# Attention outputs turned before they are normalised, border sums in four portions, and a re-ordered last head

## What is computed

```python
x = x + attention(group_norm(x, 32 groups))
x = x + conv_block(group_norm(x, 32 groups))
# attention: q, k, v = W x + b, block-diagonal over 8 heads of 16 channels;
#   softmax(q^T k / 4) over 1024 x 1024 positions in each head; times v; projection Wp, bias bp
# conv_block: depthwise 7 x 7 convolution, padding 3, bias; LayerNorm over the 128 channels
#   (gain, shift); dense 128 -> 512, exact GELU, dense 512 -> 128
```

## Time and profile before

| | |
|---|---|
| median of three runs | 354.29 us |
| profiled execution, and its span | 350.4 us, 348.6 us |
| TensorE busy | 312.3 us (90%) |
| VectorE busy | 262.3 us (75%), of it 150.6 in the maxima, 24.5 in reciprocals from SBUF |
| ScalarE busy | 174.3 us (50%) |
| GpSimd busy | 89.8 us (26%) |
| mean granted TensorE clock | 0.926 |
| chain of waits | TensorE 54%, VectorE 32%, GpSimd 6% |

### The profile page before, as it was taken

How to read it: one execution, slowest core, us unless ns; L and a number is a source line. 1 busy time by engine, 2 the same in 40 slices (tenths; PEclk the granted TensorE clock), 3 DMA queues, 4 the chain that set the end, 5 groups by cost and what they waited for, 6 DMA issues and landing times.

```text
span 348.6 us, 5518 instructions
## 1 busy us (share of the span) xinstructions
PE 312.3 (90%) x2095; PEld 139.4 (40%) x2095; DVE 262.3 (75%) x273; ACT 174.3 (50%) x347; POOL 89.8 (26%) x96
## 2 busy tenths in 40 slices
PE   7999999938999999997699799799997899997896
PEld 3453644413454454452244344344333343422232
DVE  2758759845989989987498778998997239997621
ACT  1315548724877777765367447677325262201132
POOL 6102262991000000000005175978401010100110
PEclk9999859985999999999889659999999599999999
DMA  6273011211221232123011223770000002641001
GB/s 197 48 120 84 1 24 25 37 19 19 37 53 23 37 53 39 24 50 53 0 26 31 47 87 56 176 148 8 5 8 0 0 8 57 147 113 69 0 5 56
DMA packets 10538, 17.34 MB, mean 50 GB/s; under 512 B 3588, under 2 KB 5764, under 8 KB 10512
## 3 DMA queue, kind: packets, MB, share of 16 engines
q1 hardware_dynamic: 10320, 16.60, 22.0%
q10 hardware_dynamic: 192, 0.39, 0.7%
HBM read 5.00 MB, written 1.73 MB: 19 GB/s over the span
## 4 chain that ended last, share of the span: by engine, by line
PE 54%; DVE 32%; POOL 6%; issue 3%; DMA 2%; ACT 2%; SPq 1%; DVEq 0%; POOLq 0%
PE ps L1022 13%; PE ps L1033 13%; DVE mx L738 13%; PE ps L978 7%; DVE hl L782 6%; DVE rden L748 5%; PE ps L1121 4%; POOL inside L531 4%; DVE on L750 3%; PE ps L928 2%; PE ps L954 2%; PE ps L1186 2%; PE ps L1200 2%; PE ps L1145 2%; ACT pr L654 1%
## 5 line engine op out<-in xcount | busy, mean ns | idle before, releaser
L738 DVE TENSOR_REDUCE mx<-ps 128x1 f32<-128x1024 f32 x128 | 150.6, 1218 | 36.5 <-PE ps L978 36.2
L654 ACT ACTIVATE pr<-ps 128x512 f32<-128x512 f32 x256 | 134.8, 600 | 77.2 <-PE ps L1022 76.8
L1022 PE MATMUL ps<-qs,ks 50*128 50x512 f32 x256 | 104.5, 473 | 9.8 <-DVE xs L764 4.0
L978 PE MATMUL ps<-ks,qs 48*128 48x512 f32 x256 | 102.9, 471 | 5.6 <-DVE mx L738 5.6
L1033 PE MATMUL ps<-pr,va 128*32 128x256 f32 x1024 | 77.1, 424 | 0.0
L1022 PEld LDWEIGHTS ps<-qs,ks 50*128 50x128 f32 x256 | 46.8, 201 | 64.7 <-ACT pr L654 34.3
L978 PEld LDWEIGHTS ps<-ks,qs 48*128 48x128 f32 x256 | 45.4, 199 | 21.8 <-DVE mx L738 15.4
L1033 PEld LDWEIGHTS ps<-pr,va 128*32 128x32 f32 x1024 | 28.4, 117 | 36.2 <-ACT pr L654 15.4
L500 POOL CAST mparts<-mx 128x8 fp32r<-128x8 f32 x16 | 3.1, 191 | 152.3 <-DVE mx L738 152.3
L782 DVE SCALAR_TENSOR_TENSOR hl<-xpad,w,hl 128x512 f32<-128x512 f32 (+1 forms) x43 | 40.1, 934 | 1.2
L1121 PE MATMUL ps<-xr,wt 128*32 128x512 f32 x256 | 29.5, 595 | 1.6 <-DMA xr<-xpad 1.6
(11 more groups left out here) (97 smaller groups left out, 213.2 us busy)
## 6 DMA issues: line engine op xcount, KB each, us to landing
qs<-hl SPq DMA_DIRECT2D x48, 64.0 KB, 2.4
ks<-hl SPq DMA_DIRECT2D x42, 64.0 KB, 2.4
xr<-xpad SPq DMA_DIRECT2D x16, 95.0 KB, 2.1
xr<-pad_dram SPq DMA_DIRECT2D x4, 361.0 KB, 5.8
xr<-pad_dram SPq DMA_DIRECT2D x4, 304.0 KB, 5.2
xr<-xpad SPq DMA_DIRECT2D x16, 76.0 KB, 2.1
oc<-on SPq DMA_DIRECT2D x60, 16.0 KB, 1.8
xs<-x SPq DMA_DIRECT2D x2, 256.0 KB, 3.1
```

The source lines that it names most:

```text
L654: nc.scalar.activation(pr[:, n % PR, c * HALF:(c + 1) * HALF], bank("half", n, c), ACT.Exp, scale=SCALE).then_inc(exp_done, 1)
L738: nc.vector.tensor_reduce(mx[:, s % 2, i:i + 1], sm[(NT * s + i) % 2], AX.X, ALU.max).then_inc(max_done, 1)
L978: last = nc.tensor.matmul(sm[k % 2][:, c * HALF:(c + 1) * HALF], qs[rows, cell_of(s) + i * P:cell_of(s) + (i + 1) * P], ks[rows, cell_of(s ...
L1022: nc.tensor.matmul(bank("half", n, c), ks[rows, cell_of(t) + j * P:cell_of(t) + (j + 1) * P], qs[rows, cell_of(t) + c * HALF:cell_of(t) + ...
```

## The change

- **Normalising.** `denominators` becomes `turn_u`: two transposes of 128 x 128 put positions on the partitions, so that `rden` has 8 numbers a partition and the product is 128 x 128 elements, written in `ot` (positions x channels). `spread`, `wlast`, `on`, `collect` and their transfers go.
- **Image 0's projection.** Two more uses of banks, ("oc", 0) at (8, 6) and ("oc", 1) at (9, 0): four transposes each of `ot`, copied by ScalarE into `oc`. The projections stand at (9, 2) and (9, 6); ScalarE empties them with the bias. GpSimd adds x in `pad_image` and copies the sum to `x1`.
- **Border sums.** The 14 additions come in four portions, after `split_max` of 2, 3, 4 and 5.
- **Taps of image 0.** TensorE does 8 runs instead of 7 (16 pieces in head 14 instead of 14), VectorE 9 taps instead of 12.
- **Head 15.** `centre_out` at j = 1 (was 3), `ln_var` at 3 (was 6), `ln_turn` at 5 (was 7), `ln_scale` at 7 (was after the head). VectorE applies the scale before it normalises head 15. Three of the eight half blocks of the first dense layer stand between the last head and the projection of image 1, which is now eight transposes, two copies and two matmuls.
- **Three more `keep_busy` matmuls** after each of the first two blocks of head 0.
- **Image 1.** Eight of the 32 `fill_directly` transfers go to ScalarE's queue; VectorE's taps around `conv_sum(1)`, `ln_diag(1)` and `ln_apply(1)` are cut in other portions.

```diff
-PE_RUNS = (7, 9)
-DVE_TAPS = (12, 17)
+PE_RUNS = (8, 9)
+DVE_TAPS = (9, 17)
-FINISH = {(HEADS + 1, 0): ("proj", 0), (HEADS + 1, 2): ("proj", 1), (T - 2, 5): ("mean",), (T - 1, 0): ("var",)}
+FINISH = {(HEADS, 6): ("oc", 0), (HEADS + 1, 0): ("oc", 1), (HEADS + 1, 2): ("proj", 0), (HEADS + 1, 6): ("proj", 1),
+          (T - 2, 5): ("mean",), (T - 1, 0): ("var",)}
...
             def pad_image():
...
-                nc.gpsimd.tensor_copy(inner, image(x1[:, 0, :])).then_inc(S("xpad", 0), 2)
+                nc.gpsimd.tensor_tensor(inner, image(xs[:, 0, :]), image(oc[:, 0, :]), ALU.add).then_inc(S("xpad", 0), 2)
+                g.wait_ge(S("xpad", 0), 2)
+                nc.gpsimd.tensor_copy(image(x1[:, 0, :]), inner).then_inc(S("x1", 0), 1)
...
             split_max(2)
-            taps_inside()
-            for s in range(3, HEADS + 4):
+            taps_of_rows()
+            split_max(3)
+            taps_inside(0, 3)
+            split_max(4)
+            taps_inside(3, 6)
+            split_max(5)
+            taps_inside(6, KS)
+            for s in range(6, HEADS + 4):
                 split_max(s)
...
+            def copy_oc(c):
+                a.wait_ge(S("ot_T", 0), c + 1)
+                nc.scalar.activation(oc[:, 0, c * HALF:(c + 1) * HALF], bank("oc", c), ACT.Copy).then_inc(S("oc", 0), 1)
+
+            def copy_proj(c):
+                a.wait_ge(S("bout"), 1)
+                a.wait_ge(S("projp", 0), c + 1)
+                nc.scalar.activation(oc[:, 0, c * HALF:(c + 1) * HALF], bank("proj", c), ACT.Identity, bias=bout[:, 0:1])\
+                    .then_inc(S("projected"), 1)
...
-            also = {T - 1: {4: lambda: ln_square(0), 5: lambda: ln_centred(0)}}
+            also = {HEADS: {6: lambda: copy_oc(0)}, HEADS + 1: {0: lambda: copy_oc(1), 2: lambda: copy_proj(0), 6: lambda: copy_proj(1)},
+                    T - 1: {2: lambda: ln_square(0), 3: lambda: ln_centred(0)}}
...
             copy_u(T - 1)
-            gelus(0)
+            gelus(0, 0, 1)
+            a.wait_ge(S("ot_T", 1), 1)
+            nc.scalar.activation(oc[:, 1, 0:HALF], lower[:, 0:HALF], ACT.Copy).then_inc(S("oc", 1), 1)
+            gelus(0, 1)
+            fill_directly(nc.scalar, 1, range(SHIFTS // 2, SHIFTS))
...
-                nc.vector.reciprocal(rden[:, r, :], den_of(t)).then_inc(rd_ready, 1)
+                nc.vector.reciprocal(rden[:, r, :, :], otp_of(t)[:, :, :, D]).then_inc(rd_ready, 1)
                 v.wait_ge(rd_ready, t + 1)
-                nc.vector.tensor_tensor(on[:, r, :], u[:, r, :], rden[:, r, :], ALU.mult).then_inc(ot_done, 1)
+                nc.vector.tensor_tensor(
+                    ot[:, :, t * D:(t + 1) * D].rearrange("p (q k) d -> p q k d", k=2),
+                    otp_of(t)[:, :, :, 0:D],
+                    rden[:, r, :, :].rearrange("p q (k a) -> p q k a", a=1).broadcast_to([P, 4, 2, D]), ALU.mult).then_inc(ot_done, 1)
...
-            def denominators(t):
+            def turn_u(t):
                 t_.wait_ge(u_ready, t + 1)
-                t_.wait_ge(S("spread"), 1)
-                nc.tensor.matmul(ut_of(t), spread[:, :], u[:, t % 2, :], start=True, stop=True).then_inc(ot_ready, 1)
+                for i in range(2):
+                    last = nc.tensor.transpose(ut_of(t)[:, i * P:(i + 1) * P], u[:, t % 2, i * P:(i + 1) * P], ident)
+                last.then_inc(ot_ready, 1)
...
+                    if n < 2:
+                        keep_busy(3)
...
-                if kind == "proj":
-                    for r in range(2):
-                        t_.wait_ge(S("collected", r), 64 * HEADS // 2)
+                if kind == "oc":
+                    t_.wait_ge(ot_done, HEADS)
+                    for i in range(NT // 2):
+                        last = nc.tensor.transpose(bank("oc", *of)[:, i * P:(i + 1) * P], ot[:, of[0] * NT // 2 + i, 0:P], ident)
+                    last.then_inc(S("ot_T", 0), 1)
+                elif kind == "proj":
+                    t_.wait_ge(S("oc", 0), of[0] + 1)
...
-            head(T - 2, [(5, first_bias)] + [(3 + n // 3, *quads[n]) for n in range(2 * units)])
-            head(T - 1, [(3, centre_out, 0), (6, ln_var, 0), (7, ln_turn, 0)])
+            head(T - 2, [(5, first_bias)] + [(3 + n * 5 // (2 * units), *quads[n]) for n in range(2 * units)])
+            head(T - 1, [(1, centre_out, 0), (3, ln_var, 0), (5, ln_turn, 0), (7, ln_scale, 0)])
             times_v(NT * T - 2)
             times_v(NT * T - 1)
...
+            mlp(0, 0, 0)
+            turn_u(T - 1)
+            mlp(0, 0, 1)
             t_.wait_ge(ot_done, T)
...
+            for i in range(NT):
+                last = nc.tensor.transpose(lower[:, i * P:(i + 1) * P], ot[:, i, P:2 * P], ident)
+                if i % (NT // 2) == NT // 2 - 1:
+                    last.then_inc(S("ot_T", 1), 1)
+            mlp(0, 1, 0)
+            for c, done in enumerate((S("oc", 1), S("oc_low"))):
+                t_.wait_ge(done, 1)
+                nc.tensor.matmul(lower[:, c * HALF:(c + 1) * HALF], vec(C_WP, P), oc[:, 1, c * HALF:(c + 1) * HALF],
+                                 start=True, stop=True).then_inc(S("projp", 1), 1)
+            mlp(0, 1, 1)
             mlp(0, 2)
+            mlp(0, 3)
             gn_pe_mean(t_, B + 1)
```

More of the change, by code:

```diff
@@ L159, in build @@
         us = sb("us", [P, 2, 2 * P])
[L160 to L163 removed]
+        rden = sb("rden", [P, 2, 4, 2])
+        ot = sb("ot", [P, NT, T * D])
         rowsums = sb("rowsums", [P, SIDE, KS])
@@ L328, in gn_vareps, with gn_shift @@
                 .then_inc(S("gn_ve"), 1)
+        def gn_shift(v, n):
+            rs, mean = gn_tiles[n][5:7]
+            v.wait_ge(S("gn_rstd"), n + 1)
+            nc.vector.tensor_scalar(nshift[:, n - B:n - B + 1], mean[:, 0:1], rs[:, 0:1], -1.0, ALU.mult, ALU.mult)\
+                .then_inc(S("gn_shift"), 1)
         def gn_apply(v, n, source, dest, done):
@@ L366, in x1_rows, with ends, fill_directly @@
             return (image(x1[:, 0, :]) if b == 0 else inner)[:, lo // SIDE:hi // SIDE, :]
+        def ends(b, h):
+            return ((0, TOP[b] * WIDE), (TOP[b] * WIDE, (SIDE + PE_ROWS[b] - 1) * WIDE))[h]
+        def fill_directly(queue, h, shifts):
+            lo, hi = ends(1, h)
+            queue.wait_ge(S("xpad", 1), h + 1)
+            for half in range(2):
+                queue.wait_ge(S(f"conv{half}", 0), 1)
+            for s in shifts:
+                for g in range(GROUPS):
+                    queue.dma_start(xr[s * CG:(s + 1) * CG, g, lo:hi], xpad[g * CG:(g + 1) * CG, lo + s:hi + s])\
+                        .then_inc(S(f"rep{h}", 1), 16)
         @block.sync
@@ L465, in _ @@
                     fill(0, 1)
-            collect(T - 2)
-            for h in range(2):
-                fill_directly(1, h)
+            fill_directly(sp, 0, range(SHIFTS))
+            fill_directly(sp, 1, range(SHIFTS // 2))
             for k, (b, lo, hi) in enumerate(OUTPUTS):
@@ L544, in taps_inside @@
                            .broadcast_to([P, hi - lo, KS]))
-                for d in range(KS):
+            def taps_inside(first, end):
+                for d in range(first, end):
                     lo, hi = valid(d)
@@ L758, in head @@
                         also[j]()
-            def residual(c):
-                v.wait_ge(S("projp", 0), c + 1)
-                cols = slice(c * HALF, (c + 1) * HALF)
-                nc.vector.scalar_tensor_tensor(out=x1[:, 0, cols], in0=bank("proj", c), scalar=bout[:, 0:1], in1=xs[:, 0, cols],
-                                               op0=ALU.add, op1=ALU.add).then_inc(S("x1", 0), 1)
             def conv_taps(k, lo, hi=None):
@@ L859, in _ @@
                 maxima(*divmod(k, NT))
-            also = {HEADS + 1: {1: lambda: residual(0), 3: lambda: residual(1)}}
             for t in range(T - 2):
-                head(t, also.get(t, {}))
+                head(t)
             for k in range(NT * (T - 2) + AHEAD, NT * T):
@@ L1210, in _ @@
             times_v(NT * T - 1)
-            for r in range(2):
-                t_.wait_ge(S("collected", r), 64 * (HEADS - r))
-            for c in range(2):
-                nc.tensor.matmul(lower[:, c * HALF:(c + 1) * HALF], w[0:LAST, C_WP:C_WP + P],
-                                 oc[0:LAST, 1, c * HALF:(c + 1) * HALF], start=True, stop=False, skip_group_check=True)
-            denominators(T - 1)
-            ln_scale(0)
-            t_.wait_ge(ot_done, T)
-            t_.wait_ge(S("wlast"), 64)
@@ L1228, in _ @@
+            mlp(0, 1, 1)
             mlp(0, 2)
+            mlp(0, 3)
             gn_pe_mean(t_, B + 1)
-            mlp(0, 3, 0)
-            mlp(0, 3, 1)
             mlp_down(0, 0)
+            mlp_down(0, 1)
             gn_pe_var(t_, B + 1)
-            for f in range(1, FC):
+            for f in range(2, FC):
                 mlp_down(0, f)
```

85 lines of the change are left out of this document (21 added, 64 removed).

## The result

The kernel with the change takes **320.31 us** in the median of four runs (319.2 to 326.15), against 352.84 for the kernel before in the same comparison (349.03 to 362.22): a ratio of 0.914, 95% interval 0.903 to 0.924. It is faster. The medians are over all executions, while a ratio leaves out those more than 1.5% above the kernel's quickest. The prediction had 328, range 317 to 341. The profiled execution took 319.35 us where that of before took 350.4: 31.0 less; the prediction's sum had 23.0.

What follows compares the result with a forecast made beforehand. Bound by VectorE's late maxima at head changes, otherwise the TensorE-ScalarE bank loop, plus holes from waits and low clock. Terms summed to -23.0 us, from 350.4 to 327.4 profiled; median forecast 328 us, range 317 to 341.

Steps and rivals of the forecast that it cites:

- an even part and a few holes: Even: heads 3 to 7, 12.24 us each at full clock; holes: where TensorE's clock falls, all but the first after waits.
- Normalising: 13 head changes lose VectorE's 0.72 (9.4), TensorE saves 2.8, locked products cost 3.4: net 8.8 us gained (5 to 12).
- The lock: VectorE's product held up by GpSimd's additions: two heads lose 0.72, four beside GpSimd's taps 0.5 each; 3.4 us back.
- Border sums: GpSimd's additions delay head 3's maxima, idling TensorE 6.40 us, then slow clock; portions gain 8.0 us (7 to 8.5).
- Image 0's projection: Heads 8 to 9: 9.2 us lost by a bank VectorE empties; new work 3.4; net 5.8 gained (3.5 to 6.5).
- Heads 10 to 13: 8.1 us lost after a locked product and fallen clock; 6.5 gained (1 to 8), GpSimd's pace 0.5 lost (0 to 2).
- Head 0: Extra unused matmuls gain net 1.7 us if they hold the clock, else cost 1.5 to 3; taken as 0.
- Heads 14 and 15: Stage gets longer: two convolution pieces 1.8, VectorE 0.7 gained, after y 4.6 later; together 5.6 us lost (0 to 8).
- Rivals 1 and 4: 1: clock still falls between heads 9 and 13, 337, chance 0.12; 4: VectorE doesn't set head's pace, 337, chance 0.04.
- Rival 2: The end is worse: y waits, then low clock lasts over more work; 3 to 5 us more, 332; alone 0.08.
- Rival 3: Attention: two transposes a head and shorter VectorE work keep the clock down; 396 us over 12 heads; chance 0.02.
- the rule beside it: Trainium skill's rule, cited for the attention: transposes don't count as busy for TensorE's clock as matmuls do; no size given.

Runs made afterwards that it cites:

- first experiment: The changed kernel with the old 256-wide reciprocal put back on VectorE in every head, into a tile nobody reads: 347.9 us.
- second experiment: The kernel before with one edit, GpSimd's border sums in four portions: 346.69 us.
- last experiment: The changed kernel with VectorE normalising from PSUM, image 0's old taps, head 15 in the old places and 5 unused matmuls before y: 316.67 us.

## Why the prediction was right, and where it wasn't

**What bounded the kernel.** Right: an even part and a few holes. The three behind waits, in heads 2 to 3, 8 to 9 and 10 to 13, were priced as the wait with a clock behind it, and all three closed.

**Normalising.** The 0.92 a head (0.72 on VectorE, 0.2 on TensorE) came out as 0.90 in the even heads. By the experiments the parts are 0.8 and 0.26, and they overlap: with the long reciprocal in, the shorter turn on TensorE is worth 0.09. The lock was priced at 0.72 and 0.5 a head; it cost 0.45 to 0.8, in two heads beside the border sums and three beside the taps.

**Border sums.** Predicted 8.0; alone, they gave 8.3.

**Image 0's projection.** The mechanism was the one that was named: putting VectorE back brought the 2.01 us wait, once for each half. The term came out 0.8 too large. TensorE's own added work is eight transposes at 0.66 for four and two projections at 1.12 each, 3.56, against 3.4 predicted. By the marks, before lost 8.9 over two heads of 12.24 (33.37 in all), not the 9.2 of the other ruler, and the changed kernel has 3.9 over two of its even heads (26.56 less 22.67) where 3.4 were put. That is the 0.8: 0.3, 0.2 in TensorE's work, and 0.3 that no run isolates.

**Heads 10 to 13.** The term that was mis-sized most: 6.5 predicted, with a range to 8, and the stretch gave 10.2 in all where the terms had 7.3. The prediction let a part of the low clock stay, and 0.5 for GpSimd's pace. None stayed: the clock is at 1.00, marks 11 to 12 take 11.00, and GpSimd doesn't set the pace (without the locks marks 12 to 14 are as short as the even heads). What was off in its working is the comparison "a locked pair is at worst 0.3 + 2.55 = 2.9 us, little over the old unlocked one of 2.2". The pair was at most 2.1 us (0.19 + 1.90), shorter than the old unlocked one, and TensorE then waited 0.41 at most. Even at 2.65, in the experiment with VectorE at the projection, it waited 0.83 and the clock stayed. The first experiment shows the other side: one more reciprocal, a wait of 1.04, and the clock is lost for much of what is left of the attention.

**Head 0.** Put at 0 for want of a row. Marks 0 to 2 came to 2.1 less (26.04 to 23.90), 0.3 of it by the shorter turn. The low clock there comes and goes in the code without the unused matmuls; they cost 1.5, and where it would have stayed up (22.69, second experiment) that is a loss. They are worth 1.15 net where it falls (25.05 without them); the rest of what this row shows is luck in the trace of before.

**Heads 14 and 15.** Right in sign, 2.9 too large. The two pieces cost 1.7 (1.8 predicted). The way from `gn_vareps` to y became 1.76 shorter, not 0.7. The wait for y at `centre_out` became 4.10 from 3.24, where 2.6 more were expected, since y came earlier. From y to the padded rows it became 2.7 longer, not 4.6. The prediction kept the clock of before, 0.78. At full clock before would have taken some 15.5 us there (0.78 x 19.84, an estimate that takes TensorE as the limit) and the changed kernel takes 21.0 with the gap filled. So the added work is 5.5, and 2.8 of it was given back by a clock of 0.93 in this execution. At the 29 to 30 us of other traces this stretch would have been 9 to 10 longer than before: that the row lies on the good side is luck of the execution. The remark that the interleaved LayerNorm might remove waits was right: the last experiment prices it at 3.6 us.

**Rivals.** Rivals 1 and 4 fell: no fall of the clock between heads 9 and 13, and VectorE did set the pace. Rival 2 (y waits and the low clock lasts over more work) fits the executions at 326 to 328. Rival 3 fell: with two transposes a head, and with four, the clock stays at 1.00 through the attention. What the rule beside it would have done here did not happen; whether transposes count less for the clock isn't settled by it, since they are a small part of a head.

**Slips in the working.** Rival 2 with rival 1 and GpSimd's pace is 337 + 3 to 5 + 2 = 342 to 344, not 344 to 348. The parts for heads 14 and 15 add up to 5.7, not 5.6. The chances listed outside the range add up to 0.10, not 0.15. None moves the forecast.

## What to carry to other kernels

Price a stall twice: as the time of the wait, and as the clock that may be lost behind it. Here a reciprocal of 1.75 us was worth 0.8 us in an even head, and 4 to 7 us in each of three heads of one trace where a locked product met it, so the thing to remove is the one that lets two delays meet. Where a product of two SBUF inputs on VectorE met GpSimd's work, reading one input from PSUM took the lock away. The wait of TensorE for y was worth filling with unused matmuls; filling it with the two blocks of real work instead, in the last experiment, opened a wait of 2.21 further down and lost 3.6 us. And read a gain from the stretch that was edited: the one after y took 22.6 to 31.3 us with the same work in it, by its clock.

## What the runs showed of the hardware

- **Waits and the clock.** The clock fell after a wait of 1.04 us, of 1.49, of 2.01 and of 2.21. It did not in the changed kernel's attention, where no gap is over 0.41. The length of a wait alone doesn't decide it: after one of 0.83 (VectorE at the projection) the clock stayed, after one of 1.04 late in image 1 it stayed in all twelve traces that have it, and after the wait for image 1's fill (2.3 to 2.5 us) it fell in three of twelve. After the 4.10 us `centre_out` ran slow in all eight profiles with that wait (3.59 to 3.78 us instead of 1.98), and the time until the clock was back cost between 1.6 and 10 us.
- **VectorE.** A reciprocal of 128 x 8 takes 0.14 to 0.21 us, one of 128 x 256 1.75. A product of 128 x 128 takes 0.29 free and up to 2.45 locked (1.90 in the changed kernel).
- **Transposes.** Two more in each head change nothing in the clock of the attention and cost 0.11 us each.
